# Roots, keys and gelus of a two-layer decoder kernel put in another order

## The reference

```python
x = x + attention_16_heads_of_128(layernorm(x))                      # alibi, causal
x = x + cross_attention(layernorm(x), ctx, mask)                     # 16 heads of 16, own layernorm on the delta
x = x + h_bitlinear(silu(bitlinear(ln, gate)) * bitlinear(ln, up))   # ln = layernorm(x); h_: Walsh-Hadamard first
x = x + grouped_attention(layernorm(x))                              # over the batch axis, 4 kv heads
x = x + layernorm(layernorm(x) + mean_over_time(scan(ctx)))          # one summary row for each sequence
x = x + gelu(round(layernorm(x) @ W1.T / 0.1) * 0.1) @ W2.T          # tanh gelu
```

## Time and profile before

| | us |
|---|---|
| median of 3 runs | 501.37 (501.33 to 501.39) |
| the profiled execution | 500.37 |
| its span, first to last instruction | 498.6 |
| PE busy in it | 475.3 (95%) |
| DVE busy | 365.3 (73%) |
| ACT busy | 321.6 (65%) |

### The profile page before, as it was taken

The page is one execution under the profiler, slowest core; times in us unless marked ns, Lnnn a source line. Parts: engine busy times, 40 slices in busy tenths (PEclk is TensorE's granted clock), DMA queues, the critical chain, the costliest instruction groups (busy, mean ns, idle before and its releaser), DMA issues.

```text
span 498.6 us, 16397 instructions
## 1 busy us (share of the span) xinstructions
PE 475.3 (95%) x7061; PEld 406.9 (82%) x7067; DVE 365.3 (73%) x820; ACT 321.6 (65%) x591; POOL 4.2 (1%) x15
## 2 busy tenths in 40 slices
PE   7999999999989999999999999899999999896897
PEld 7999999999878888878888888788888788684575
DVE  5576887887658755567966579966969975798973
ACT  4677787877566666677566566666667556445644
POOL 1000000000000000000000000000000000000000
PEclk9999999999999999999999999999999999988999
DMA  6376452200501211111111111111111100000000
GB/s 201 108 254 203 168 166 84 64 23 28 206 1 45 79 50 44 44 44 44 44 44 44 44 44 44 44 44 44 42 44 44 44 3 3 3 1 0 1 11 28
DMA packets 12236, 30.86 MB, mean 62 GB/s; under 512 B 1666, under 2 KB 4867, under 8 KB 11396
## 3 DMA queue, kind: packets, MB, share of 16 engines
q1 hardware_dynamic: 11716, 29.08, 18.2%
q0 software_dynamic: 192, 0.51, 0.3%
q10 hardware_dynamic: 256, 0.23, 0.1%
HBM read 29.35 MB, written 0.46 MB: 60 GB/s over the span
## 4 chain that ended last, share of the span: by engine, by line
PE 69%; DVE 20%; ACT 5%; issue 4%; DMA 1%; DVEq 0%; ACTq 0%
PE psb L1461 10%; PE psb L1451 9%; PE psa L1370 8%; PE psa L1522 8%; PE psb L1540 6%; PE psa L1383 4%; PE pst L1392 4%; PE psb L1423 3%; PE psa L1403 2%; ACT shared L628 2%; DVE shared L998 1%; DVE st L782 1%; PE pst L1607 1%; DVE scratch L972 1%; PE psb L1414 1%
## 5 line engine op out<-in xcount | busy, mean ns | idle before, releaser
L1461 PE MATMUL psb<-wkv,cx 128*125 128x256 f32 x576 | 80.3, 288 | 2.7 <-DVE kx L1004 2.7
L1451 PE MATMUL psb<-cx,wkv 128*128 128x500 f32 x276 | 74.5, 405 | 0.8 <-ACT vmem L471 0.8
L1461 PEld LDWEIGHTS psb<-wkv,cx 128*125 128x125 f32 x576 | 71.0, 186 | 4.9 <-DVE kx L1004 3.0
L471 ACT ACTIVATE vmem<-psb 125x512 f32<-125x512 f32 x45 | 26.8, 596 | 50.1 <-PE psb L1461 49.8
L1451 PEld LDWEIGHTS psb<-cx,wkv 128*128 128x128 f32 x276 | 48.3, 188 | 12.6 <-ACT vmem L471 1.1
L1522 PE MATMUL psa<-qb,kx 32*125 32x112 f32 x1536 | 54.7, 279 | 0.8 <-ACT shared L628 0.6
L998 DVE TENSOR_SCALAR shared<-shared,top 125x896 f32<-125x896 f32 x48 | 30.8, 683 | 32.8 <-ACT shared L628 32.6
L1522 PEld LDWEIGHTS psa<-qb,kx 32*125 32x125 f32 x1536 | 46.3, 183 | 8.3 <-issue 3.5
L628 ACT ACTIVATE shared<-psa 125x1792 f32<-125x1792 f32 x24 | 40.0, 1668 | 17.4 <-PE psa L1522 17.2
L1370 PE MATMUL psa<-cx 128*128 128x448 f32 x192 | 44.5, 382 | 0.7 <-ACT cx L362 0.7
L628 ACT ACTIVATE smem<-psa 125x1792 f32<-125x1792 f32 x23 | 38.3, 1667 | 9.4 <-PE psa L1522 9.4
(11 more groups left out here) (350 smaller groups left out, 833.7 us busy)
## 6 DMA issues: line engine op xcount, KB each, us to landing
ring<-ctx_t_dram SPq DMA_DIRECT2D x24, 500.0 KB, 3.4
whd<-wqk_dram SPq DMA_DIRECT2D x16, 256.0 KB, 2.7
qb<-wvp_dram SPq DMA_DIRECT2D x8, 256.0 KB, 2.8
whd<-wo_dram SPq DMA_DIRECT2D x16, 128.0 KB, 2.6
wraw<-w_dram SPq DMA_DIRECT2D x2, 1024.0 KB, 5.8
mats_sb<-mats_dram SPq DMA_DIRECT2D x1, 1536.0 KB, 8.1
wraw<-gate_dram SPq DMA_DIRECT2D x1, 1024.0 KB, 6.8
wraw<-up_dram SPq DMA_DIRECT2D x1, 1024.0 KB, 6.5
```

Source lines behind the costliest of these rows:

```text
L471: nc.scalar.activation(vu[u % 2][:, 2 * r:2 * r + 2, :, 0:XD], bank[0:CT, :].rearrange("p (t h d) -> p t h d", t=2, d=XD), ACT.Copy).then_ ...
L1451: last = nc.tensor.matmul(bank[:, 0:UT], wkv[a][:, 0, c, m * P:(m + 1) * P], cx[b][u % 2][:, c, :], start=(a == b and c == 0), stop=(a == ...
L1461: last = nc.tensor.matmul(bank[0:CT, t * D:(t + 1) * D], cx[b][u % 2][:, c, a0:a0 + CT], wkv[a][:, 1, c, :], start=(a == b and c == 0), st ...
```

## The change

- In rounds 17, 29 and 41 VectorE's `take_k` stands ahead of `remainder`.
- `add_summary` moves from n = 16 to 15 in VectorE's `early`, `add_normalised` from 16 to 15 in its `late`, and `normalise7` from `early` (before clip) to `between` (behind clip) in the same round. `root(6)` moves from ScalarE's `early` at 16 to `first` at 15, `root(7)` from `late` at 16 to `first` at 17.
- In the tail ScalarE has the Relu of tile 1's hidden values ahead of the last copy of keys and values of the grouped attention, gelu(0) with its load ahead of `move_xbe(3)`, `back` behind the Identity, and gelu(1) behind `root(7, 2)` with a load of its own. gelu(2) then follows without a load, and `root(5, 3)` comes behind it and `back`. Of the warming matmuls the twelve ahead of `hidden_part(0, 0)` become two and the three behind it eight.

```diff
--- before.py
+++ after.py
@@ -586,6 +586,10 @@
                     move_y2(t)
                 if o == 14:
                     root(5, t)
+                if o == 15:
+                    root(6, t)
+                if o == 17:
+                    root(7, t)
 
             def early(t, o):
                 if o == 1:
@@ -597,8 +601,6 @@
                     move_tw(t)
                 if o == 11:
                     move_xbe(t)
-                if o == 16:
-                    root(6, t)
                 if o == 18:
                     move_x7T(t)
 
@@ -618,8 +620,6 @@
                     move_sy(t)
                 if o == 12:
                     move_aT(t)
-                if o == 16:
-                    root(7, t)
 
             def exponential(s):
                 act.wait_ge(s_qk, s + 1)
@@ -687,31 +687,31 @@
             floor_h(1)
             move_tw(3)
             root(5, 2)
+            act.wait_ge(s_zl, 2)
+            nc.scalar.activation(hz[1], hz[1], ACT.Relu, bias=low[:, 1:2], scale=-1.0).then_inc(s_zh, 1)
             act.wait_ge(s_qkv, 5)
             nc.scalar.activation(kv1[:, :, 6:8, :].rearrange("p k b e -> p b k e"),
                                  pvb[0:TT, 0:D].rearrange("p (b k e) -> p b k e", b=2, k=2), ACT.Copy).then_inc(s_kve, 1)
             root(6, 2)
+            nc.scalar.preload_act_table(ACT.Gelu_apprx_tanh)
+            gelu(0)
             move_xbe(3)
-            act.wait_ge(s_zl, 2)
-            nc.scalar.activation(hz[1], hz[1], ACT.Relu, bias=low[:, 1:2], scale=-1.0).then_inc(s_zh, 1)
             act.wait_ge(s_zh, 1)
             nc.scalar.activation(hz[1], hz[1], ACT.Identity, bias=low[:, 2:3], scale=-1.0).then_inc(s_z1, 1)
+            back()
             act.wait_ge(s_var[6], 3)
             move_sy(3)
-            nc.scalar.preload_act_table(ACT.Gelu_apprx_tanh)
-            gelu(0)
-            gelu(1)
-            back()
             softmax_exp(3)
             root(7, 2)
+            nc.scalar.preload_act_table(ACT.Gelu_apprx_tanh)
+            gelu(1)
             move_x7T(2)
             move_h(2, 0)
             move_h(2, 1)
             move_aT(3)
-            root(5, 3)
-            nc.scalar.preload_act_table(ACT.Gelu_apprx_tanh)
             gelu(2)
             back()
+            root(5, 3)
             root(6, 3)
             root(7, 3)
             nc.scalar.preload_act_table(ACT.Gelu_apprx_tanh)
@@ -1194,16 +1194,16 @@
                     weights(t)
                     attend(t)
                     gather(t)
-                if o == 16:
+                if o == 15:
                     add_summary(t)
-                if o == 17:
-                    normalise7(t)
 
             def between(t, o):
                 if o == 2:
                     add_delta(t)
                 if o == 8:
                     quantise_hidden(t)
+                if o == 17:
+                    normalise7(t)
 
             def late(t, o):
                 if o == 2:
@@ -1217,14 +1217,14 @@
                     add_down(t)
                 if o == 13:
                     add_proj(t)
-                if o == 16:
+                if o == 15:
                     add_normalised(t)
 
             for s in range(PAIRS - 2):
+                if s in BEHIND:
+                    take_k(s // 2 + 1, 1)
                 if s % 2 and s // 2 + 2 < B * UPB:
                     remainder(s // 2 + 2)
-                if s in BEHIND:
-                    take_k(s // 2 + 1, 1)
                 if s in (1, 3, 5):
                     normalise1(s // 2 + 1)
                 if s in (3, 5, 7):
@@ -1858,11 +1858,11 @@
             for c in range(DC):
                 last = nc.tensor.matmul(A1[0:TT, 0:D], xbe[:, c, :], mats_sb[:, WOUT, c, :], start=False, stop=(c == DC - 1))
             last.then_inc(s_sy, 1)
-            keep_warm(12)
+            keep_warm(2)
             pe.wait_ge(s_kve, 7)
             hidden_part(0, 0)
             hidden_part(0, 1)
-            keep_warm(3)
+            keep_warm(8)
             turn_x7(2)
             keep_warm(1)
             hidden(2, 0)
```

## The result

The changed kernel takes 505.2 us (median of 4 runs, 504.75 to 506.61) against 501.35 before: 1.0084 of it, 95% interval 1.0063 to 1.0105. It is slower, and the time lies in the range; a second set of six executions, beside a kernel before of 501.17, gave 505.52, ratio 1.0086 (1.0069 to 1.0103). The profiled execution took 504.75 us, its span is 502.9.

What follows compares the result with a forecast made beforehand. VectorE was taken as the bound around round 28, its queue from take_k to craw stopping TensorE. Loop +4.3 and tail -0.7 gave +3.6 us; clock falls of 1.5 and 1.7 made +6.8, so 508.2 us, range 503.8 to 510.6.

Steps and rivals of the forecast that it cites:

- Part A: Rounds 17 to 19: the remainder behind take_k moves VectorE's queue by 1.1 us, craw comes late, TensorE loses 0.8 us.
- Part B, the new stop: Rounds 27 and 39: root(6) holds ScalarE until the variance, xqT comes late, TensorE stops 2.1 us before gate_up.
- Part B, what a site costs: Late keys with the remainder behind them delay craw and the ring load: 1.6 us at site one, 1.9 at site two.
- Part C, the gain at tile 3: Tail: gelu(2) finds its table and root(6, 3) is freed; TensorE gains 0.35 before hidden_part(2), 0.4 before turn_x7(3): 0.8 us.
- The clock in the tail: After a new 2.5 us TensorE stop before xbe's product, the clock likely falls to 1.2 GHz on hidden_part(0), costing 1.5 us.
- The clock at the loop sites: After each 2.1 us stop before gate_up, the clock falls with even odds, 1.7 us each; one fall counted.
- The sum: Whole kernel: +3.6 us with the clock held, plus 1.5 in the tail and 1.7 at one loop site: +6.8, 508.2 us.
- rival 1: Whole kernel: the stops come but the clock holds everywhere, 505.0 us; chance 0.19.
- Rival 2: Round 28's VectorE overload is spread, stops of 1.49 and 1.23 us go, the tail gives 0.7: 498.0 us; chance 0.06.
- Rival 3: ScalarE isn't held up, keys come earlier, but craw and the ring load come when they did: about 501.2 us; chance 0.05.

Runs made afterwards that it cites:

- the remainder first: The changed kernel with the remainder ahead of the keys again, as before the change: 503.8 us, ratio 1.0057 to the kernel before.
- the roots alone: Kernel before with only the roots, add_summary, add_normalised and normalise7 moved as in the change: 504.34 us, ratio 1.0047.
- the filled stops: Kernel before with the roots and VectorE's steps moved, plus eight warming matmuls in TensorE's stops ahead of gate_up of rounds 27 and 39: 501.71 us, ratio 1.0010.
- the roots alone with root(6) late: Kernel before with the roots and VectorE's steps moved, but root(6) in ScalarE's late list and the remainder ahead of the keys: 500.86 us, ratio 1.0003.

## Why the prediction was right, and where it was not

- **Part A, 0.8 us in rounds 17 to 19: right.** +0.83; weighted_values(18) waited 0.74 us for craw. Every kernel with the keys first in round 17 shows +0.82 to +0.84, every other one 0.02 or less.
- **Part B, the new stop: right, a little large.** 1.84 and 1.85 us where I had 2.1: xqT and the shorter copy overlap the root and each other by more than I gave them (306.22 - 305.29 = 0.93 from the root's start to xqT's end, not 1.1). ScalarE's wait was 3.50 us. The order on ScalarE is its cause, shown by root(6) in the late list.
- **Part B, what a site costs: right.** 1.56 for 1.6, and 1.72 (second set 1.54) for 1.9. The argument that craw moves by the keys' lateness and the remainder holds: without the remainder behind the keys it is 0.43 us. The second site waits for the ring load in both profiles, in the second set for craw as well; its size is blurred by when the load lands.
- **Part C, the gain at tile 3: mis-sized.** From turn_x7(2) to turn_x7(3) it is 492.07 - 476.98 = 15.09 us against 487.68 - 471.35 = 16.33: -1.24, where I had -0.8. From the start of hidden_part(1) to the warmers it is 6.90 us instead of 7.73 (484.28 to 491.18, and 478.70 to 486.43), where I had 0.35, and from there to turn_x7(3) 0.89 instead of 1.25, where I had 0.4. The trace of before shows three of the four warmers, so some 0.2 us may belong to the second part and not the first; the sum is not touched by that.
- **The clock in the tail: right.** 1.48 us for 1.5. But the kernel before's own low stretch at 453.5 to 456.9, which I carried over unchanged, does not come in the changed kernel's profile. The columns 46-end are -0.77 with and -0.07 without that luck (second set, where it came).
- **The clock at the loop sites: the step that failed in size.** I took one fall of 1.7 us as the likely case, and the total, 508.2, hung on it. In both profiles of the changed kernel it held at both sites. It does fall there in the profile with the remainder first, where it cost 1.5 us, and the upper group of the roots alone (7 of 12 executions), which the filled stops removed, is put down to it. How often it falls in the changed kernel itself is not known.
- **The sum.** 505.2 is next to rival 1 (505.0, the clock held everywhere), and that is luck, since its condition wasn't met: the tail's clock did fall. With that fall and none in the loop my terms give 501.4 + 3.6 + 1.5 = 506.5. Of the 1.3 us between, tile 3 gave 0.4 more and the loop sites cost 0.2 less than I had; the rest is about as much as a low stretch more or less in the tail moves a single profile, and I can't place it. Rival 2, the relief, did not come. Rival 3 describes the changed kernel with root(6) late, and that one took 503.23 us and not 501.2: craw did not come when it did, it came a microsecond later, as the remainder lay behind late keys. What is right in it is that moving VectorE's work forward is worth nothing (the roots alone with root(6) late, 1.0003).
- **The pages.** The load's row in the changed kernel is 1.28 us again, with ScalarE's next instruction 0.02 us behind it (485.49 after 484.19 + 1.28), so this case shows no drain of the kind that the Trainium skill (ScalarE: Activation LUTs, What ACT_TABLE_LOAD costs) adds. And stops of 1.84 and 2.49 us were followed by 1.2 GHz, shorter ones than those that the Trainium skill (TensorE: Matmul & The Clock Gate, Why this matters for your kernels) warns of.

Left open: which executions have the clock fall in the loop, why the upper group of the roots alone is 2.4 us higher and not 1.5, and what sets the first 20 us. The kernel before itself took between 499.5 and 502.6 us, and I have not taken that apart.

## What to carry to other kernels

When a step is moved to an earlier slot, look at what stands behind its wait in that engine's list: a root of 0.5 us placed 3.5 us before its input was ready held three copies and through them TensorE. A long instruction that nobody waits for (here the remainder) costs nothing while it lies in its engine's wait, and its whole length once it stands behind that wait. When an engine's whole queue between two of its readers is the bound, moving work inside the queue gains nothing; what gains is to put the few instructions that others wait for (here the keys, the weigh that frees a ring slot, craw) ahead of the long ones that nobody waits for. A new stop on TensorE also has a price through the clock, and it comes in a part of the executions only, so it has to be looked for in the spread of the times as well as in a profile.

## What the runs showed of the hardware that I had not expected

The last ring load of 500 KB lands 4.2 us after the instruction that frees its slot in one profile and 5.4 us in another of a kernel that is equal up to there; over all profiles it is 3.4 to 5.4 us. And a stop of 1.85 us before gate_up split the executions of one kernel into two groups 2.4 us apart, which eight matmuls that nobody reads made one again.
